# Output matmuls of both streams ahead of the scores in an attention loop, and bf16 layer norm statistics

## The reference

```python
Q = jnp.einsum('bse,hed->bhsd', x, Wq) + bq[None, :, None, :]      # K, V alike
scores = jnp.einsum('bhsd,bhtd->bhst', Q, K) * scale
scores = jnp.where(causal[None, None], scores, -jnp.inf)
w = jax.nn.softmax(scores, axis=-1)
o = jnp.einsum('bhst,bhtd->bhsd', w, V)
x = _layernorm(x + (o @ Wo + bo))
h = jax.nn.silu(gate) * up                                         # gate, up = x @ wg.T, x @ wu.T
x = _layernorm(x + jnp.einsum('bsh,dh->bsd', h, wd))
```

## Time and profile before

| | us |
|---|---|
| median of 2 runs | 2335.33 |
| these runs | 2322.76 and 2347.9 |
| the profiled execution | 2110.53 |
| span of its slowest core (core 3) | 2109.0 |

### The profile page before, as it was taken

How to read it: one execution, slowest core, us unless ns; L and a number is a source line. 1 busy time by engine, 2 the same in 40 slices (tenths; PEclk the granted TensorE clock), 3 DMA queues, 4 the chain that set the end, 5 groups by cost and what they waited for, 6 DMA issues and landing times. The chain is left out here.

```text
span 2109.0 us, 24738 instructions; the slowest of 8 cores (2100.4 to 2109.0 us)
## 1 busy us (share of the span) xinstructions
PE 1755.7 (83%) x9056; PEld 679.6 (32%) x9056; DVE 681.0 (32%) x792; ACT 913.2 (43%) x1142; POOL 93.9 (4%) x181
## 2 busy tenths in 40 slices
PE   1279897997998998979979985977599996799992
PEld 1144232352232432323522321321244442344440
DVE  1223254314351342543143513354212114322115
ACT  0013867926958648679269585111111103111103
POOL 2100000000000000000000000000111100011000
PEclk9689897998998998979989987889799998899996
DMA  8911000001000010000000002600344400444002
GB/s 142 140 30 21 1 1 11 1 1 21 1 11 1 1 21 1 1 11 1 1 1 1 1 1 41 120 0 0 60 73 69 79 1 9 111 81 80 1 1 80
DMA packets 30804, 64.65 MB, mean 31 GB/s; under 512 B 3808, under 2 KB 3936, under 8 KB 30048
## 3 DMA queue, kind: packets, MB, share of 16 engines
q0 software_dynamic: 25376, 52.44, 15.3%
q1 hardware_dynamic: 5312, 10.63, 1.5%
HBM read 107.10 MB, written 8.39 MB: 55 GB/s over the span
## 5 line engine op out<-in xcount | busy, mean ns | idle before, releaser
L388 ACT ACTIVATE PT<-pp 128x1024 bf16<-128x1024 f32 x640 | 628.0, 1025 | 188.8 <-PE pp L377 182.3
L399 DVE TENSOR_TENSOR PT<-PT,masks_sb 128x1024 bf16<-128x1024 bf16 x256 | 308.2, 1224 | 380.1 <-ACT PT L388 379.8
L419 PE MATMUL pso<-PT,V 128*64 128x512 bf16 x640 | 268.3, 419 | 51.0 <-DVE PT L399 33.4
L373 PE MATMUL pp<-Q2T,K2T 64*128 64x512 bf16 x640 | 262.0, 413 | 54.4 <-ACT PT L388 46.4
L422 PE MATMUL pso<-PT,V 128*64 128x512 bf16 x640 | 272.3, 425 | 0.0
L377 PE MATMUL pp<-Q2T,K2T 64*128 64x512 bf16 x640 | 263.2, 415 | 0.0
L428 PE MATMUL psd<-PT,onescol 128*1 128x512 bf16 x640 | 253.0, 395 | 0.0
L426 PE MATMUL psd<-PT,onescol 128*1 128x512 bf16 x640 | 252.9, 395 | 0.0
L296 PE MATMUL pp<-wv_sb,xT 128*128 128x256 bf16 x1024 | 136.2, 277 | 15.7 <-DMA wv_sb<-wv 12.7
L419 PEld LDWEIGHTS pso<-PT,V 128*64 128x64 bf16 x640 | 69.2, 108 | 215.4 <-issue 215.4
L373 PEld LDWEIGHTS pp<-Q2T,K2T 64*128 64x128 bf16 x640 | 58.9, 94 | 228.6 <-issue 228.6
(11 more groups left out here) (102 smaller groups left out, 1839.1 us busy)
## 6 DMA issues: line engine op xcount, KB each, us to landing
wgb<-wg POOLq DMA_DIRECT2D x48, 256.0 KB, 5.0
wub<-wu POOLq DMA_DIRECT2D x48, 256.0 KB, 5.8
stg<-x POOLq DMA_DIRECT2D x32, 256.0 KB, 15.2
y<-y SPq DMA_DIRECT2D x4, 2048.0 KB, 6.9
wd_sb<-wd POOLq DMA_DIRECT2D x4, 1536.0 KB, 11.0
stg<-xq POOLq DMA_DIRECT2D x16, 256.0 KB, 11.8
masks_sb<-mk SPq DMA_DIRECT2D x1, 2048.0 KB, 12.2
wq_sb<-wq POOLq DMA_DIRECT2D x8, 256.0 KB, 4.0
```

The source lines that it names most:

```text
L373: e.matmul(pp[par][:, 0:512], K2T[0:64, kc * 128:(kc + 1) * 128], Q2T[0:64, t * 512:(t + 1) * 512], start=True, stop=True)
L388: pool_cons.append(st('act', lambda e, par=par, gpt=gpt: e.activation(PT[:, gpt, :], pp[par][:], AF.Exp, scale=SCALE), waits=exp_waits, in ...
L399: msnap = st('dve', lambda e, gpt=gpt, t=t, rel=rel: e.tensor_mul(PT[:, gpt, :].rearrange("p (h q) -> p h q", h=2), PT[:, gpt, :].rearrang ...
L419: e.matmul(ps_o[opar][0:64, :], V2[:, kc, ppar * 128:ppar * 128 + 64], PT[:, gpt, 0:512], start=first, stop=last)
```

## The change

In the attention loop, the outputs of both streams are issued at the head of iteration j, ahead of both scores. The first of them takes the waits of both: both exponentials or masks of j-2, and, for chunk 0, both normalisations. In stage 2, ScalarE copies each chunk of y1 to bf16 (new buffers yb_sb) ahead of the Square, which now writes bf16, and both sums are bf16 matmuls; the evacuation into y1 now waits for ScalarE's reads instead of the matmuls'.

```diff
             for j in range(nmax + 3):
+                pk = j - 2
+                pv_tasks = [(t, t % 2, nkc) for (t, nkc) in streams
+                            if 0 <= pk < nkc]
+                pv_first = True
+                for (t, opar, nkc) in pv_tasks:
+                    pvw = []
+                    if pv_first:
+                        for (t2, opar2, nkc2) in pv_tasks:
+                            pvw.append(pv_ready[(t2, pk)])
+                            if pk == 0:
+                                pvw += [('s_dve_on', last_on[opar2]),
+                                        ('s_dve_rs', last_rs[opar2])]
+                        pv_first = False
+                    def pvmm(e, ...):   # the same four matmuls
...
+                    pv_done[(t, pk)] = st('pe', pvmm, waits=pvw, inc=('s_pe_pv', 1))
+
                 for (t, nkc) in streams:
...
-                    pk = j - 2
-                    if pk < 0 or pk >= nkc:
-                        continue
-                    pv_waits = [pv_ready[(t, pk)]]
-                    if pk == 0:
-                        pv_waits += [('s_dve_on', last_on[opar]),
-                                     ('s_dve_rs', last_rs[opar])]
...
-                    pv_done[(t, pk)] = st('pe', pvmm, waits=pv_waits, inc=('s_pe_pv', 1))
...
-    sq_sb = s_p2.enter_context(nc.sbuf_tensor('sq_sb', [128, 2, 512], F32))
+    yb_sb = s_p2.enter_context(nc.sbuf_tensor('yb_sb', [128, 2, 512], BF16))
+    sq_sb = s_p2.enter_context(nc.sbuf_tensor('sq_sb', [128, 2, 512], BF16))
...
-                waits=[('s_pe2', wo_user[par]), y1_free[qp]],
+                waits=[('s_pe2', wo_user[par]), ('s_act2', y1_free[qp])],
...
+            st('act', lambda e, ec=ec, par=par, lp=lp: e.activation(
+                yb_sb[:, par, :], y1[:, lp, ec, :], AF.Copy),
+                waits=[('s_dve2', evacs[(lq, ec)]), ('s_pe2st', yb_free[par])],
+                inc=('s_act2', 1))
             asnap = st('act', lambda e, ec=ec, par=par, lp=lp: e.activation(
                 sq_sb[:, par, :], y1[:, lp, ec, :], AF.Square),
-                waits=[('s_dve2', evacs[(lq, ec)]), ('s_pe2st', yb_free[par])],
                 inc=('s_act2', 1))
...
-                e.matmul(pstat_s[:], onesrf[:, 0:1], y1[:, lp, ec, :],
+                e.matmul(pstat_s[:], onescol[:], yb_sb[:, par, :],
                          start=(ec == 0), stop=(ec == NEC - 1))
-                return e.matmul(pstat_q[:], onesrf[:, 0:1], sq_sb[:, par, :],
+                return e.matmul(pstat_q[:], onescol[:], sq_sb[:, par, :],
                                 start=(ec == 0), stop=(ec == NEC - 1))
...
-        y1_free[lp] = ('s_pe2st', mk.c['s_pe2st'])
+        y1_free[lp] = mk.c['s_act2']
```

More of the change, by code:

```diff
@@ L364, in build_full, with pvmm @@
             for j in range(nmax + 3):
+                pk = j - 2
[11 more added lines that the diff above has]
+                        pv_first = False
+                    def pvmm(e, kc=pk, opar=opar, gpt=slot_of[(t, pk)], ppar=ppar,
+                             nkc=nkc):
+                        first, last = kc == 0, kc == nkc - 1
+                        e.matmul(ps_o[opar][0:64, :],
+                                 V2[:, kc, ppar * 128:ppar * 128 + 64],
+                                 PT[:, gpt, 0:512], start=first, stop=last)
+                        e.matmul(ps_o[opar][64:128, :],
+                                 V2[:, kc, ppar * 128 + 64:ppar * 128 + 128],
+                                 PT[:, gpt, 512:1024], start=first, stop=last,
+                                 tile_position=(0, 64), skip_group_check=True)
+                        e.matmul(ps_den[opar][0:1, :], onescol[:], PT[:, gpt, 0:512],
+                                 start=first, stop=last)
+                        return e.matmul(ps_den[opar][64:65, :], onescol[:],
+                                        PT[:, gpt, 512:1024], start=first, stop=last,
+                                        tile_position=(0, 64), skip_group_check=True)
+                    pv_done[(t, pk)] = st('pe', pvmm, waits=pvw, inc=('s_pe_pv', 1))
                 for (t, nkc) in streams:
@@ L502, in build_full @@
     evacs = {}
-    y1_free = [('s_pe2st', 0), ('s_pe2st', 0)]
+    y1_free = [0, 0]
     for qt in range(5):
@@ L537, in build_full, with stmm @@
             par = ec % 2
+            st('act', lambda e, ec=ec, par=par, lp=lp: e.activation(
+                yb_sb[:, par, :], y1[:, lp, ec, :], AF.Copy),
+                waits=[('s_dve2', evacs[(lq, ec)]), ('s_pe2st', yb_free[par])],
+                inc=('s_act2', 1))
             asnap = st('act', lambda e, ec=ec, par=par, lp=lp: e.activation(
                 sq_sb[:, par, :], y1[:, lp, ec, :], AF.Square),
[L540 removed]
                 inc=('s_act2', 1))
[L543 to L544 removed]
+            def stmm(e, ec=ec, par=par):
+                e.matmul(pstat_s[:], onescol[:], yb_sb[:, par, :],
                          start=(ec == 0), stop=(ec == NEC - 1))
[L546 removed]
+                return e.matmul(pstat_q[:], onescol[:], sq_sb[:, par, :],
                                 start=(ec == 0), stop=(ec == NEC - 1))
```

## The result

The change makes the kernel slower: ratio 1.0626, 95% interval 1.0594 to 1.0658. The median after is 2250.58 us (9 runs), and before it is 2123.44 us over 8 runs. The profiled execution after took 2248.01 us, the span of its slowest core (again core 3) 2246.5 us, against 2110.53 and 2109.0 before: +137.5 us.

A forecast was written before the change was run, and what follows sets the result against it. TensorE was taken to set the pace in two-stream iterations, ScalarE having 0.05 us of slack a unit. Terms 79 + 19 + 15 - 21 = +92 us on the median 2335.33 gave 2427 us, range 2365 to 2490.

The forecast's parts named there:

- the step "Sum": Last step: 79, 19, 15 and -21 us, together +92, put on the shown median 2335.33, giving 2427 us.
- the two-stream term: Attention iterations with both streams: loop through ScalarE makes them 2.12 us (2.16 masked) against 1.94; +38 us, counted at half, 19.
- the starts: Starts of tile pairs: second ones 2.2 us later, waiting for both normalisations, first ones gaining 0.3; +15 us in all.
- The masked stretch of one stream: Stream B's last 8 masked units per tile pair: 3.69 us loop spans two units, not three; 4.9 us, 16 times, +79 us.
- the second rival: TensorE's clock falls in the one-stream stretches, 2.17 us a unit, 41 us more: 2468 us; chance 0.13.
- a granted clock of 0.5: Sign in the profile after that the forecast is wrong: TensorE granted only this clock in the one-stream stretches.
- it stayed at 1.00 for 16 us with only 34 matmuls: Argument against a falling clock in one-stream stretches: full clock held with one matmul every 0.47 us.
- The sum of 4.25 us: Attention iterations with both streams: score-to-exponential loop through ScalarE and score buffers takes this long for two iterations, 2.12 us each.
- the lower bound, "nothing": Starts of tile pairs: no loss if the clock rises as early as before; the upper bound was 8 x 4.4.
- The statistics: Stage 2 layer norm: bf16 blocks of 7.6 us instead of 13.7, three saving 6.1, the fourth only 2.3; -21 us.
- The rule on tiling modes: Two-stream iterations: mode changes drain TensorE, so halving them should gain; the forecast saw no such term in the rows.
- the last rival: Two-stream iterations: grouped score pairs start 0.22 us apart, not 0.32, iteration 1.84 us, -22 us, total 2292 us; chance 0.04.

The follow-up runs named there:

- third: Against the kernel before: both outputs ahead of both scores only while both streams have scores, one-stream stretches and statistics as before; ratio 1.021.
- fourth experiment: Against the kernel before: output ahead of the score only where stream B is alone, two-stream iterations and statistics as before; ratio 1.0487.
- the fillers: Attention reordering with fp32 statistics, plus two extra 512-column matmuls per one-stream unit: 1.069 against the kernel before; starting only with each stretch's third unit: 1.0636.
- the half exponentials: Exponential and mask on 512 of 1024 columns, in the order before and with outputs ahead of both scores; profiled executions 2059.81 and 2086.50 us.
- the longer starts without masks: Attention reordering with fp32 statistics, mask products of the one-stream stretches left out (128 of 256); ratio 1.0264 to the kernel before.
- the reordered kernel: Against the kernel before: only the new order in the attention loop, statistics left in fp32; ratio 1.075, +159 us.

## Why the prediction was wrong

**The base, in the step "Sum".** The forecast was 2427 us and the measured time is 2250.58. This step alone moved the forecast by 205 us, from 2222. 111 us were added to a median of 2335.33 that lay 225 us above the profiled execution, and for that gap the two-stream term was halved to 19, where 35.4 were measured. The measured median before is 2123.44, 0.6% above the profiled 2110.53. On the profiled execution the text's own sum was 2222, 5.3% more; the profiled execution after took 2248, 6.5% more, and the ratio is 6.3%. The rows could not explain those 225 us, the prediction said so, and it still let them decide 200 us of its number. The step that failed is to take two runs over the one execution that every row came from. That the sum itself came within 27 us of the 137.5 is in part luck: the starts, 14 us too dear, stand against a one-stream term and projections that were 41 us too cheap.

**The masked stretch of one stream: right mechanism, term too small.** The round of 3.69 us for two units is in the trace to the hundredth. 79 us were forecast and 108.5 measured. The missing 29 us are for the most part the second rival's, the falling clock, which had 0.13 and is true together with the forecast: 4.36 us for a round at the low clock (forecast 4.34). The prediction itself named a granted clock of 0.5 in these stretches as a sign of being wrong. An estimate from the trace: 169.7 us of the stretches at the low clock, times 1 - 3.69/4.36, is 26 us. The inference that failed is "it stayed at 1.00 for 16 us with only 34 matmuls", one block of another stage. TensorE was busy 9.24 of 16 us there and 4.77 of 8 in the stretch where the clock then fell: nearly the same share. And the row ended too early. The same trace before, right behind it:

```profile
1774.31 1.71 PE L778 MATMUL pC<-mrow,onesrf 1*128 1x512 f32 x2 [2.07 <-ACT rrow L769]
```

```profile
1775.00:1784.00 9.00, 9.00 (x15) 2.81 (x14) 6.21 (x10) 1.26 (x2) 0.00 (x0) 0.50 0.00 1
```

That thin stretch was followed by the low clock too. TensorE had also paused for 2.07 us by then, so the trace does not say whether the thin work or the pause brought it down; but it is no case in which thin work left the clock alone.

**A term that was not in the sum: the projections.** +11.2 us. The prediction stopped the price of a low clock at the end of the stretch that causes it. The next matmuls at full density pay for it too. The third and fourth experiment (289.9 and 303.1 us) tie it to the one-stream stretches, and the fillers took part of it back.

**The stretches of two streams: right.** +35.4 for +38. The sum of 4.25 us, the bound for the pitch from denominator to output (0.31 us: 251.61 to 251.92) and the two scores 0.23 apart held. Only its picture of equal iterations was off, and its last product: 12 x 0.22 + 11 x 0.18 is 4.62 us, 37 in all and not 38.

**The starts: wrong size.** +1.4 for +15. The delay itself came as worked out; the second tile pair's first outputs and scores after:

```profile
232.69 0.60 PE L404 MATMUL pp<-Q2T,K2T 64*128 64x512 bf16 x1
...
245.98 0.60 PE L382 MATMUL pso<-PT,V 128*64 128x512 bf16 x1 [3.70 <-DVE o_allT L248]
...
248.16 0.60 PE L404 MATMUL pp<-Q2T,K2T 64*128 64x512 bf16 x1
...
250.09 0.40 PE L382 MATMUL pso<-PT,V 128*64 128x512 bf16 x1
```

Its first score was at 232.69, so score A(2) came at +15.5, forecast 238.78 - 223.13 = 15.65. But at 250.09, +17.4, matmuls last 0.40 us: the clock is up, and the scores of iteration 3 and all of iteration 4 run at it. Before, iteration 3 was all but done by then, and had been paid at the low clock: its scores at 237.69 and 239.32 last 0.60 us. Waiting used up low-clock time in which before work was done. The step took the delay as additional to all else. By the starts of the matmuls, the second tile pairs' first four iterations went from 138.8 to 148.4 us in all, +9.6 for +17.6, and the first tile pairs' from 71.3 to 64.5, -6.8 for -2.4. So both halves came out cheaper, and that their sum fell near the lower bound, "nothing", is luck.

**The statistics: right.** Of the 22.1 us, 19.4 lie behind the first projection matmul, for 21 forecast; the other 2.7 came from a shorter wait for the weights of stage 2, which the change doesn't touch. The fourth block behaved as read from the earlier trace rows: the row chain began at 1612.57, right behind the last apply.

```profile
1612.57 0.68 DVE L564 TENSOR_SCALAR mrow<-pstat_s 1x512 f32<-1x512 f32 x1
```

**The rule on tiling modes.** The Trainium skill, TensorEngine Tiling (Array Packing), section Key Properties, says that changing the mode drains TensorE. The trace after still shows no price for it: denominator to output, the same kind, is 0.31 us (251.61 to 251.92), denominator to score, another kind, 0.31 too (252.26 to 252.57; 0.32 before, 255.67 to 255.99). The gain of 0.09 to 0.11 us an iteration that the half exponentials uncover is that of two score pairs in a row (0.23). So the last rival's mechanism exists at the size given, and it never became visible because the loop through ScalarE is longer.

Not settled: what the clock responded to at 1774, the 3.0 us up to the first score (193.3 and 196.3; the other kernels show 191 to 199 with the same code there), the longer starts without masks, and what the fillers cost by themselves.

## What to carry to other kernels

Where engines hand work round in a ring, write down the ring's length and how many units it spans in the order of emission: the pace is the one divided by the other, and moving one group of instructions ahead of another changes the divisor (here 3.69 us over three or over two units). A wait that TensorE didn't have before can be priced twice, once as itself and once as the lower clock that it leaves to the work behind it; here the waits of the one-stream stretches were, and those of the two-stream iterations (0.41 us in the rows above, TensorE busy for 28.16 of 31 us at a granted clock of 1.00) were not. And when a few shown runs disagree with the profiled execution and no row says why, forecast the ratio from the execution that the rows come from.

## What the runs showed of the hardware

- Two score pairs in the two row halves of the array, one directly behind the other, start 0.23 us apart (251.16 to 251.39), while output and denominator pairs in the column halves keep 0.31 to 0.34 us, even when their kind does not change.
- More matmuls made the kernel faster: 2 extra of 512 columns in each one-stream unit after the second brought the reordered kernel from 1.075 to 1.0636. Its 16 one-stream stretches were at the low clock for 10.5 us in all instead of 147.5.
- A row with the clock at 1.00 does not show that thin work is free: 9.24 of 16 us busy in one place and 4.77 of 8 in another were both granted 1.00, and both were followed by 0.50 (from 1774.6 us before, from 226.0 after).
